# A graph network's last layer: one-hots ahead of the next chunk's scaling on ScalarE, two groups of edge products ahead of the next hidden units on TensorE

## The reference: what is computed

```
h = relu(edge_feat @ W1 + b1)                   # 64 hidden units of each edge
w = (h @ W2 + b2).reshape(e, 4, 8, 8)           # 256 weights of each edge
s_e, v_e = x[src][:, :8], x[src][:, 8:].reshape(e, 8, 3)
m0 = 0.25*(einsum(s_e*sh0, w[:,0]) + C110*einsum(v_e, sh1, w[:,3]))
m1 = 0.25*(einsum(s_e, sh1, w[:,1]) + einsum(v_e*sh0, w[:,2]))
out = segment_sum([m0, m1], dst) + self products of x
```

## Time and profile before

| what | us |
|---|---|
| runs (lowest, median, highest of 3) | 9516.43, 9542.63, 9567.0 |
| profiled execution, span from its first to its last instruction | 5779.0 |
| of it, from the last layer's first gather to the end | 2635 |

### The profile page before, as it was taken

The page is one execution under the profiler, slowest core; times in us unless marked ns, Lnnn a source line. Parts: engine busy times, 40 slices in busy tenths (PEclk is TensorE's granted clock), DMA queues, the critical chain, the costliest instruction groups (busy, mean ns, idle before and its releaser), DMA issues.

```text
span 5779.0 us, 132934 instructions
## 1 busy us (share of the span) xinstructions
PE 4906.1 (85%) x47121; PEld 3926.4 (68%) x47122; DVE 4334.3 (75%) x8266; ACT 2952.9 (51%) x7181; POOL 4010.0 (69%) x4168
## 2 busy tenths in 40 slices
PE   7788888888888886766687999999999999999997
PEld 4487887787777775443443777777777777777775
DVE  4488887888888884111111899999999999999998
ACT  5555555555555552000001666666666666666664
POOL 0677777777777777777601777777777777777774
PEclk7556655666666666777787788888888788888887
DMA  9754455656656558999996111111111111111111
GB/s 330 291 189 179 176 189 181 223 206 235 209 205 236 207 206 296 364 364 364 340 324 177 28 28 28 28 28 30 28 28 28 28 28 30 28 28 28 30 28 20
DMA packets 596624, 865.48 MB, mean 150 GB/s; under 512 B 170817, under 2 KB 418690, under 8 KB 579458
## 3 DMA queue, kind: packets, MB, share of 16 engines
q1 hardware_dynamic: 363858, 385.79, 21.3%
q10 hardware_dynamic: 99504, 406.06, 17.9%
q0 software_dynamic: 133120, 71.57, 7.3%
HBM read 455.19 MB, written 406.85 MB: 149 GB/s over the span
## 4 chain that ended last, share of the span: by engine, by line
POOL 61%; issue 21%; DMA 9%; PE 5%; DVE 2%; ACT 1%; POOLq 0%; another core or an unknown queue 0%; ACTq 0%; SPq 0%; DVEq 0%
POOL gathered L614 61%; DMA arena<-adj 5%; PE psum L1088 2%; DMA rel_table<-arena 1%; DMA arena<-counts 1%; PE psum L1058 1%; DMA table_out<-adj 1%; PE psum L952 1%; ACT table_out L666 0%; PE psum L894 0%; ACT arena L666 0%; PE psum L921 0%; DMA gathered<-rel_table,idx 0%; DMA idx<-key_i 0%
## 5 line engine op out<-in xcount | busy, mean ns | idle before, releaser
L614 POOL DMA_INDIRECT gathered<-x_rows,idx x2048 | 1943.7, 949 | 903.1 <-issue 624.6
L614 POOL DMA_INDIRECT gathered<-rel_table,idx x2048 | 2001.4, 977 | 637.9 <-issue 636.3
L1177 PE MATMUL psum<-w,arena 65*128 65x256 f32 x4096 | 1198.4, 444 | 1.9 <-DVE arena L1826 1.9
L1177 PEld LDWEIGHTS psum<-w,arena 65*128 65x128 f32 x4096 | 889.7, 225 | 274.4 <-issue 144.3
L739 ACT COPY arena<-psum 128x512 f32<-128x512 f32 x1024 | 603.0, 589 | 855.8 <-PE psum L1002 794.8
L952 PE MATMUL psum<-arena 128*128 128x184 f32 x4096 | 887.7, 376 | 8.9 <-DVE acc L1539 8.9
L952 PEld LDWEIGHTS psum<-arena 128*128 128x128 f32 x4096 | 853.4, 235 | 45.5 <-issue 9.6
L952 PE MATMUL psum<-gathered,arena 128*128 128x32 f32 x4096 | 703.5, 343 | 206.2 <-DMA gathered<-rel_table,idx 206.2
L952 PEld LDWEIGHTS psum<-gathered,arena 128*128 128x128 f32 x4096 | 692.9, 267 | 234.0 <-issue 151.1
L853 ACT ACTIVATE arena<-gathered,sh 128x32 f32<-128x32 f32 x2048 | 448.1, 307 | 528.4 <-DMA gathered<-x_rows,idx 528.4
L1826 DVE TENSOR_TENSOR arena<-psum,arena 128x256 f32<-128x256 f32 x1536 | 671.2, 492 | 0.0
(11 more groups left out here) (223 smaller groups left out, 5297.0 us busy)
## 6 DMA issues: line engine op xcount, KB each, us to landing
adj<-arena ACTq DMA_DIRECT2D x128, 2048.0 KB
arena<-adj SPq DMA_DIRECT2D x93, 2048.0 KB
counts<-arena ACTq DMA_DIRECT2D x128, 512.0 KB
arena<-counts SPq DMA_DIRECT2D x64, 1024.0 KB, 11.5
arena<-adj SPq DMA_DIRECT2D x40, 1024.0 KB
rel_table<-table_out ACTq DMA_DIRECT2D x32, 1024.0 KB, 9.9
rel_table<-arena ACTq DMA_DIRECT2D x32, 1024.0 KB, 10.0
gathered<-rel_table,idx POOLq DMA_INDIRECT x2048
```

The source lines that it names most:

```text
L614: pool.indirect_dma_start(gathered[:, s, j, :], None, rows[l], bass.IndirectOffsetOnAxis(ap=idx[:, s, j:j + 1], axis=0),).then_inc(rows_in ...
L1177: mm = pe.matmul(pair[g % 2][:, WN * q:WN * q + WN], hidden[:, s % 2, q, P * g:P * g + P], w2[:, :], start=True, stop=True)
```

## The change

ScalarE: in `beside`, the one-hots of chunk c come before the scaling of chunk c+1 instead of after it. TensorE: in `chunk3`, the hidden units of chunk c+1 come behind the edge products of group 1 instead of group 0, still ahead of the first part of the scatter. No instruction is added or removed.

```diff
@@ -858,8 +858,9 @@
                 if following:
                     hidden_units(c + 1, s + 1)
+                onehots(3, c, s)
+                if following:
                     scale_rows(c + 1, (s + 1) % SLOTS, it if s + 1 < SLOTS else it + 1)
-                onehots(3, c, s)
@@ -1184,7 +1185,7 @@
                 for g in range(GROUP):
                     edge_weights(c, s, g)
-                    if g == 0 and following:
+                    if g == 1 and following:
                         hidden_units(c + 1)
                     if prev and g >= 1:
                         if g == 1:
```

## The result

Nine runs of the changed kernel have a median of 9465.44 us (9430.83 to 9511.84), nine of the kernel before beside them 9533.65 us (9502.2 to 9580.1).

A forecast was written before the change was run, and what follows sets the result against it. POOL's gathers were taken to bound the last layer at 20.06 us a chunk: 0 x 128 in the steady part, 8 us gained in the tail, so 9542.6 - 8 = 9534.6 us, called "no change"; range 9504 to 9567.

The forecast's parts named there:

- these 3763.6 us: Runs' median above the profiled span; no row shows it, the change gives it no reason, so it was kept unchanged.
- the 8 us: Gain taken for the last layer's tail, near the slow end of 7.7 to 11.9 us; span from 5779.0 to 5771.
- 20.06 us of gathers stay: Last layer, steady part: POOL's 16 gathers at 1.254 us each set every chunk's time, which the change leaves alone.
- 0 x 128: Steady part of the last layer: no gain in any of its 128 chunks.
- My bound of 25 us: Last layer: consumers could be 25 us later before POOL noticed, less the latency of the small index load.
- They fit and 3.9 us are left: ScalarE's new round in the last layer: copy and ReLUs 5.8, one-hots 6.9, scaling 3.5, in all 16.2 of 20.06 us.
- The one-hots' wait: ScalarE's one-hots of chunk c wait until VectorE has added chunk c-2; costed at nothing.
- TensorE and VectorE in the tail: Last layer's end: VectorE begins chunk 127 about 2 to 6.2 us after its landing, not 13.9; gain 7.7 to 11.9 us.
- The rival that TensorE becomes the bound: Last layer: more TensorE work at 1.2 GHz costs 2.1 us a chunk beyond what is left, 267 us, 9809; chance 0.05.
- The rival on the faster side: Timed runs not bound by gathers: consumers bring a last-layer chunk from 20.06 to 19.2 us, 109 us, 9434; chance 0.05.

The follow-up runs named there:

- the kernel with indices ahead: ScalarE's part alone, plus last-layer source indices loaded a round earlier into a second set of four slots, against the kernel before: 5777.88 us (0.9992), 5778.09 (0.9995), 5781.74 (0.9995).

## Why the prediction was wrong, and where it was right

**The step that failed** is the one between the span and the median: "The runs' median lies 3763.6 us above that span, in which I see no row and to which the change gives no reason". I took these 3763.6 us as something that lies around the kernel and carried them over unchanged. They were 39% of the time to be predicted. The one row set I had was of another kind of execution, with another limit in the last layer, and the 8 us worked out from it were added to a time that it doesn't describe. What the runs showed in its place: own time and span differ by 1.8 to 2.0 us in every execution of either kind; the 3.7 ms are longer rounds, with a standstill in each, 3554 of 3683 us of them in the two layers with gathers; and the change takes 68 us, the parts alone 85 and 51 in a set of runs in which before was 166 us faster.

**POOL's pace.** "20.06 us of gathers stay" and "0 x 128" hold in the short kind (20.08 us a chunk after), as far as a few us can be told: the 2048 gathers take 2570.3, 2574.1 and 2577.4 us in the three traces of the change against 2568.3 in the one of before. In the long kind the burst of 19.9 us stays too, but it isn't the round: 31.7 us before, of which the 11.7 behind the burst belong to the consumers. My bound of 25 us before POOL would notice a later consumer came from the earlier trace rows, and in the long kind it is gone: POOL waits for indices in nearly every chunk, 11.7 us on average in before (1115.3 over 95), because the slot is released only when VectorE has caught up.

**ScalarE.** "They fit and 3.9 us are left": right in the short kind, where L853 is still ended by the gather, 107 times in the waits above, 3.6 us on average. The one-hots' wait was rightly costed at nothing; no wait for it appears.

**TensorE and VectorE in the tail.** Forecast: VectorE begins chunk 127 2 to 6.2 us after the landing, a gain of 7.7 to 11.9, of which I took 8. Measured: 3.9, 5.6 and 4.0 us in three traces, so 10.0, 8.3 and 10.0 us in the tail; in time 6.9, 5.2 and 1.7 us in three sets, whose intervals all hold 8 us (the narrowest side is 0.9985, which is 8.7 us). The mechanism was right and the tail's size too, it would have been a good forecast of a short execution, and in time it is small enough that the third set can't tell it from nothing. In the long kind the tail gives nothing (98.0 us against 99.1 and 98.9 with the parts).

**The rival that TensorE becomes the bound** (9809 us) did not come: the granted clock in the layer is 0.83 after and 0.82 before, in the long kind 0.65 and 0.66.

**The rival on the faster side** (9434 us, chance 0.05) is the one that came true by its first sentence: "an execution that is not spaced like the profiled one". Its second sentence was wrong. It let the consumers set a pace of 19.2 us; in the long kind the round is 31.7, the gathers bind more and not less, and the order gains because it moves work out of the stretch behind the burst. I gave it too little because I argued against it from POOL's waits in the earlier trace rows, which can say nothing of runs that are 3763.6 us longer. What the Trainium skill says and I had set beside it ("DMA: Bandwidth & Descriptors", section "Anatomy of one DMA — SWDGE (gpsimd) path", descriptor generation "small, variable") doesn't fit the traces: a gather of the last layer keeps POOL 944 to 950 ns on average, with 0.30 us behind it, in both kinds.

**The chances.** With the gap in plain sight, faster by over 0.5% should have had far more than 0.05, and slower too; the range of 63 us was that of a kernel whose limiting stage I had seen, and I had not.

## What to carry to other kernels

Compare the span of the profile with the runs' median before reading any row: if they differ by more than a few us, the rows tell of another execution than the times, and a change has to be costed for both, with a range that admits it. Where one engine issues bursts of gathers and others signal across them, the time behind a burst isn't hidden: put work that can end before it ahead of it, and count what stands between the last gather and the release of a slot. A gain of two orders in one kind of execution (0.9909, 0.9947) can be nothing worth having in the other (0.9990, 0.9998), so a result is only as good as the kind it was measured in.

## What the runs showed of the hardware that I had not expected

- The same kernel, with the same inputs, takes 5780 or 9370 us. One execution of 11 of the kernel with indices ahead took 9230.39 us among others of 5772 to 5784, and one of before 6298.82 among others of 5775 to 5788: it can change from one execution to the next, and an execution can lie between. The mean granted clock of an execution goes with the kind, 0.73 to 0.74 in the short one and 0.60 to 0.62 in the long one. The execution of 6298.82 has 0.61; that of 9230.39 is recorded with 1.00, as no other, so it may not be of the long kind.
- In the long kind, TensorE's signals to VectorE come late in a burst of gathers: in the two rounds shown 12.8 and 12.3 us after the products ended, 1.6 and 2.8 us after the last gather. TensorE is busy 94 to 100% of the first eleven gathers of a burst and 23% of the last five (before, mean of 99 rounds), and ScalarE's activations come 1.4 us apart towards the end. Without gathers in the layer this is gone. In the short kind the same gathers, at the same 0.95 us each, hold nobody back.
- A gather by POOL keeps it for 0.94 to 0.95 us and mostly 0.30 more until the next, whichever the kind: 16 of them are 19.75 us on average in the short kind and 19.9 in the long one (19.7 and 20.9 in the two rounds shown).

**What stays open.** What makes an execution long, and by which path signals and instructions are held back, no run here tells. The lower clock could be a part of the cause or only follow from TensorE's pauses. In the long kind the whole change was timed only against before, in another set of runs than its parts, so whether 85 and 51 us add up, or the whole is no better than ScalarE's part alone, isn't known; its 68 us lie between the two. The index-ahead kernel was meant to take the 2.3 to 2.5 us of the index load out of each round there, some 300 us over 128 chunks as an estimate from the rounds above; its one execution of 9230.39 us has no run of before beside it of the same kind, and a clock on record that fits neither kind. No version is shown to beat both kernels by more than the measurement can tell.
